# Tile 1 in tile 0's order of columns, another order of the first loads, and B asked earlier

## The reference

```python
w = weights[conditions]                      # per sample 64 x 64
x = x + einsum('bct,bcd->bdt', x, w)         # layer 0, over the channels
H = einsum('btd,od->bto', x, W)              # layer 1, W is 512 x 512
xa = einsum('btd,brd->btr', x, A[idx])       # rank 16, 8 adapters
delta = einsum('btr,bor->bto', xa, B[idx]) * s[idx]
x = x + H + delta
```

## Time and profile before

| | us |
|---|---|
| median of 3 runs (77.91 to 78.04) | 78.03 |
| the profiled execution | 78.45 |
| its span in the trace | 76.8 |
| TensorE busy | 71.4 |
| VectorE, ScalarE, GpSimd busy | 54.9, 51.1, 32.8 |

### The profile page before, as it was taken

One profiled execution on the slowest core, in us unless ns is written; L12 is line 12 of the kernel. 1 busy time (PEld: TensorE's weight loads), 2 busy tenths in 40 slices (PEclk: granted clock), 3 DMA queues, 4 the chain that ended last, 5 costly groups with the idle time before them and its releaser, 6 DMA issues.

```text
span 76.8 us, 1946 instructions
## 1 busy us (share of the span) xinstructions
PE 71.4 (93%) x466; PEld 65.3 (85%) x466; DVE 54.9 (72%) x144; ACT 51.1 (67%) x126; POOL 32.8 (43%) x76
## 2 busy tenths in 40 slices
PE   3996999979999999999999999999999999999940
PEld 3974888938899989999999999999999999999930
DVE  4006985386869887979598877978697959685920
ACT  0586861881997697686768676968678676667430
POOL 5700395095599934545155706570655250000000
PEclk9999999999999999999999999999999999999999
DMA  0899459157689899759956863578407430303025
GB/s 0 211 370 388 149 120 314 44 163 258 197 274 271 292 294 288 247 181 284 331 136 225 273 225 89 168 219 294 162 23 254 137 141 0 137 13 137 0 109 169
DMA packets 10238, 14.56 MB, mean 190 GB/s; under 512 B 3698, under 2 KB 5234, under 8 KB 10226
## 3 DMA queue, kind: packets, MB, share of 16 engines
q1 hardware_dynamic: 7586, 9.04, 36.7%
q0 software_dynamic: 1536, 4.20, 17.6%
q10 hardware_dynamic: 1104, 1.19, 4.9%
HBM read 10.23 MB, written 4.19 MB: 188 GB/s over the span
## 4 chain that ended last, share of the span: by engine, by line
PE 74%; DMA 13%; ACT 2%; DVE 2%; issue 2%; ACTq 2%; POOLq 0%; POOL 0%
PE z_ps L616 53%; DMA w_raw<-w_t 7%; DMA b_raw<-b_t 5%; PE out_ps L658 5%; PE out_ps L671 4%; PE out_ps L672 4%; PE out_ps L676 4%; PE v_ps L650 3%; ACT b_high L345 2%; DVE b_stack L483 1%; ACTq L291 1%; PE out_ps L664 1%; ACT x_high L352 1%; ACTq L295 1%; DVE out_sb L591 1%
## 5 line engine op out<-in xcount | busy, mean ns | idle before, releaser
L616 PE MATMUL z_ps<-moving,x_high 128*128 128x272 f32 x224 | 33.3, 289 | 0.0
L616 PEld LDWEIGHTS z_ps<-moving,x_high 128*128 128x128 f32 x224 | 29.9, 188 | 0.5
L252 POOL DMA_DIRECT2D b_raw<-b_t x32 | 16.1, 505 | 12.8 <-issue 6.2
L616 PE MATMUL z_ps<-moving,x_low 128*128 128x272 f32 x112 | 18.7, 289 | 0.0
L616 PEld LDWEIGHTS z_ps<-moving,x_low 128*128 128x128 f32 x112 | 15.8, 188 | 0.0
L245 POOL CAST moving<-a_table 128x128 fp32r x28 | 8.2, 322 | 15.1 <-PE z_ps L616 14.4
L483 DVE TENSOR_TENSOR b_stack<-b_raw,b_high 128x512 fp32r<-128x512 f32 x16 | 11.7, 734 | 2.2 <-ACT b_high L345 2.2
L474 DVE TENSOR_TENSOR z_low<-z_ps,z_high 128x272 fp32r<-128x272 f32 (+1 forms) x28 | 11.8, 421 | 1.2 <-ACT z_high L329 0.2
L345 ACT ACTIVATE b_high<-b_raw,group_sb 128x512 fp32r<-128x512 f32 x16 | 11.5, 716 | 1.4 <-DMA b_raw<-b_t 1.4
L329 ACT ACTIVATE z_high<-z_ps 128x272 fp32r<-128x272 f32 (+1 forms) x28 | 10.5, 376 | 0.1
L451 DVE TENSOR_TENSOR x_low<-x_raw,x_high 128x512 fp32r<-128x512 f32 x14 | 10.5, 751 | 0.1
(11 more groups left out here) (52 smaller groups left out, 71.1 us busy)
## 6 DMA issues: line engine op xcount, KB each, us to landing
b_raw<-b_t POOLq DMA_DIRECT2D x32, 128.0 KB, 3.3
x_raw<-xt SPq DMA_DIRECT2D x15, 256.0 KB, 4.4
out<-out_sb SPq DMA_DIRECT2D x15, 256.0 KB, 3.0
w_raw<-w_t ACTq DMA_DIRECT2D x2, 272.0 KB, 3.8
w_sb<-w SPq DMA_DIRECT2D x32, 16.0 KB, 3.2
a_scales<-a_t ACTq DMA_DIRECT2D x1, 260.0 KB, 3.9
x_raw<-xt SPq DMA_DIRECT2D x2, 128.0 KB, 3.5
w_raw<-w_t ACTq DMA_DIRECT2D x1, 240.0 KB, 5.7
```

The source lines that it names most:

```text
L252: pool.dma_start(b_raw[s * C:(s + 1) * C, t % BBUFS, :], b_t[ds(which[s], 1), :, :].rearrange("a r (g n) -> (a r) g n", g=1) .to_broadcast ...
L616: last = nc.tensor.matmul(z_bank(t, part), x[:, t % XBUFS, k * P:(k + 1) * P], moving[:, int(n == HL), k, at:at + HALF], start=((n, k) == ...
```

## The change

Tile 1 now uses tile 0's layout (`side(t)` is 0 for both plain tiles): its A columns stand right of W and its A bank is bank 1. The columns right of W in `w_raw` therefore serve tile 0 and then tile 1, and `take_raw_a(1)` waits for tile 0's A bank to be done. TensorE's order becomes tile 0 W, tile 1 W, tile 0 A, two thirds of w_bank(2), weigh_low_rank(0), the last third, tile 1 A, out of tile 0, weigh_low_rank(1), a_bank(2). ScalarE's queue issues W 0, W 1, x(1), A; W piece 2 goes to SyncE's queue in x(1)'s place. GpSimd's first request for B waits for W piece 1 instead of piece 2. On ScalarE and VectorE the order of the steps in the opening follows.

```diff
@@ side and banks
+        def side(t):
+            return 0 if t < PLAIN else t % 2
-            return A_BANK[t % 2] if part == A_PART else 1 - A_BANK[t % 2]
+            return A_BANK[side(t)] if part == A_PART else 1 - A_BANK[side(t)]
...
@@ SyncE
-            load_x(1)
+            load_w(2)
             load_w(3)
             load_x(2)
...
@@ GpSimd
-            pool.wait_ge(w_loaded[2], 16)
+            pool.wait_ge(w_loaded[1], 16)
             load_b(which[0], 0)
...
@@ ScalarE
             load_w(0)
+            load_w(1)
+            act.dma_start(x_raw[:, 1, :], xt[1]).then_inc(x_loaded[1], 16)
             act.dma_start(a_scales[:], a_t).then_inc(a_loaded, 16)
-            load_w(1)
-            load_w(2)
...
-                at = 0 if t % 2 else AC + OUT
+                at = AC + OUT
+                if t:
+                    act.wait_ge(plain_bank_done[t - 1], 1)
...
             high_of_w(0)
-            act.wait_ge(a_loaded, 16)
-            take_raw_a(1)
-            take_raw_a(0)
             high_of_w(1)
             take_z(0, W_PART)
+            act.wait_ge(a_loaded, 16)
+            take_raw_a(0)
             high_of_w(2)
             high_of_x(2)
             high_of_w(3)
+            take_z(1, W_PART)
             act.wait_ge(a_scaled_ready, 1)
             nc.scalar.activation(a_table[:, :, 0, :], a_scaled[:], ACT.Copy).then_inc(a_high_ready, 1)
-            take_z(1, A_PART)
+            take_raw_a(1)
             take_z(0, A_PART)
+            high_of_v(0)
             act.wait_ge(groups_ready, 2)
             high_of_b(0)
+            high_of_z(2, W_PART)
             high_of_x(3)
             high_of_b(1)
-            take_z(1, W_PART)
-            high_of_v(0)
+            take_z(1, A_PART)
+            high_of_w0(BATCH_OF[2])
             high_of_v(1)
-            high_of_z(2, W_PART)
-            high_of_w0(BATCH_OF[2])
+            take_out(0)
...
-            take_out(0)
             take_out(1)
@@ VectorE
+            low_of_x(2)
             low_of_w(2)
-            low_of_x(2)
+            low_of_w(3)
             dve.wait_ge(own_rank_ready, 2 + PER)
-            take_low_rank(1)
-            low_of_w(3)
             take_low_rank(0)
...
+            low_of_v(0)
             low_of_b(0)
+            low_of_z(2, W_PART)
+            take_low_rank(1)
             low_of_b(1)
-            low_of_v(0)
-            low_of_v(1)
-            low_of_z(2, W_PART)
             low_of_x(3)
             low_of_w0(BATCH_OF[2])
+            low_of_v(1)
@@ TensorE
             pe.wait_ge(x_loaded[1], 16)
+            plain_products(1, W_PART, by_row).then_inc(w_bank_done, 1)
             pe.wait_ge(raw_cols_ready, PER)
-            plain_products(1, A_PART, by_row).then_inc(plain_bank_done[1], 1)
-            pe.wait_ge(raw_cols_ready, 2 * PER)
             pe.wait_ge(w_loaded[2], 16)
             plain_products(0, A_PART, by_row[:K // 2])
...
             plain_products(0, A_PART, by_row[-1:]).then_inc(plain_bank_done[0], 1)
-            plain_products(1, W_PART, by_row).then_inc(w_bank_done, 1)
 
             pe.wait_ge(z_plain_ready[0], 1)
             pe.wait_ge(w_low_ready, 2)
-            w_bank(2, 0, K)
+            w_bank(2, 0, 2 * K)
             weigh_low_rank(0)
-            w_bank(2, K, 2 * K)
+            w_bank(2, 2 * K, 3 * K)
+            pe.wait_ge(raw_cols_ready, 2 * PER)
+            plain_products(1, A_PART, by_row).then_inc(plain_bank_done[1], 1)
+            plain_layer0(0)
             weigh_low_rank(1)
-            w_bank(2, 2 * K, 3 * K)
-            plain_layer0(0)
```

8 lines of the change are left out of this document (4 added, 4 removed).

## The result

| | before | changed |
|---|---|---|
| median, 20 runs each, us | 78.55 (77.91 to 79.71) | 78.06 (77.31 to 78.89) |
| the profiled execution | 78.45 | 77.90 |
| its span | 76.8 | 76.2 |
| start of weigh_low_rank(0) (behind one third of w_bank(2) in before, behind two in the changed kernel) | 13.79 | 12.13 |
| end of a_bank(2) | 18.72 | 17.78 |

Changed over before is 0.994, with a 95% interval of 0.9912 to 0.9969: faster by 0.49 us, where 1.21 was forecast. The ratio and its interval leave out the executions that took over 1.5% more than the fastest of their kernel; the medians take in all 20. These runs of before have their median at 78.55 and not at the 78.03 of the first three, so the time to set beside the forecast is the gain, not the 76.8.

What follows compares the result with a forecast made beforehand. TensorE's chain was taken as the bound, through W's and B's transfers before 17.24 us. Ending a_bank(2) at 17.51 instead of 18.72 saves 1.21 us, so 78.03 becomes 76.8 us; forecast 76.5 to 77.1, range with rivals 76.1 to 77.7.

Steps and rivals of the forecast that it cites:

- What bounds the kernel; the head: Opening: TensorE idles 1.46 and 0.91 us before a_bank(2) ends; W's second piece before A gains 1.09 us at third matmul.
- A's columns: After tile 1's W bank: A lands at 8.05, so TensorE waits 0.47 us, from 8.40 to 8.87; bounds 0 and 0.9.
- Part 3: Chain through ScalarE and VectorE to tile 0's mask: TensorE idles 0.32 us; an earlier A lengthens this wait.
- The chain to weigh_low_rank(0): x(2), high, low, two low W pieces, then mask: weigh_low_rank(0) starts at 11.97, within 11.65 to 12.2.
- rival 1: In the head, early B pushes x(2) by 0.65 us: gain 0.6, time 77.4 us; chance 0.14.
- From there to the end of a_bank(2): From weigh_low_rank(0), TensorE needs 5.54 us, no work added or saved, so a_bank(2) ends at 17.51 instead of 18.72.
- The 0.91 of B and v(0) is gone because both are early.: TensorE's 0.91 us idle before tile 0's low-rank product vanishes because SyncE and GpSimd are asked a piece sooner.
- What stays put: After the opening: GpSimd's work for tiles 2 and 3 moves up by up to 0.9 us; nothing lost later.
- rival 2: GpSimd doesn't move, ScalarE waits for the identity of tiles 4 and 5: 0.45 given back, 77.3 us; chance 0.13.
- The signal named for it: Sign listed as proving the forecast wrong: TensorE has gaps between 22 and 27 us; no size given.
- Rivals 4 and 5: Head: B starves A, 78.2 us, chance 0.10 including no change; or x(1) held back, at most 0.3 us, no own chance.
- rival 3: A lands early (7.6), weigh_low_rank(0) at 11.65 or 11.4: gain 1.5 to 1.8, 76.4 us; chance 0.11.

Runs made afterwards that it cites:

- best kernel: Changed kernel with VectorE's mask of tile 0 before its last two low W pieces and B asked at W's third piece: 77.26 us (0.9854), again 77.68 (0.9879).
- the experiment with the old loads: Changed kernel with the first loads issued in the order of the kernel before, all else changed: 78.20 us, 0.9965 of before.
- the kernel with B late: Changed kernel with GpSimd's first request for B waiting for W's third piece again, as in before: 77.74 us, 0.9913 of before.
- the kernel with the casts on purpose: Changed kernel with GpSimd's casts from tile 6 on released just ahead of VectorE's subtraction, to make them collide: 78.13 us, 0.9958 of before.
- the kernel in which GpSimd waits: Changed kernel with GpSimd waiting for VectorE's subtraction of tile 3 before it takes tile 5's A columns: 77.60 us, 0.9907 of before.

## Why the prediction was off, step by step

- **What bounds the kernel; the head.** Right in what it rests on: the second W piece landed at 5.24 (forecast 5.25), the third matmul is at 5.70, as forecast, and from there tile 0's and tile 1's W banks run without a gap. One reading under it is wrong: the first two matmuls of before were not through at 5.33 with 1.46 us lost. Their four records start at 4.43, 5.04, 5.49 and 5.76, since the clock rose only at 5.56; the row itself names 0.63 us of idle time. The 0.449 us for a matmul is the price at full clock alone. The 1.09 us from third matmul to third matmul stand, but for these two executions: in before the W piece came at 6.33 (7.00 and 7.41 in two others of the old order), and in the changed kernel the clock had risen by 4.43. In the best kernel's second profile, where it rose at 7.25, the third matmul starts at 6.49 with nothing but the pace ahead of it. By the medians the experiment with the old loads comes out at 78.20 against 78.06, which is hardly less gain. The sum had no term for the clock.
- **A's columns.** Mis-sized to the good side: A landed at 7.67, not at 8.05, inside the bound "in the middle of its slot". No stall near 8.4; the first products of w_bank(2) start at 10.21 with no idle time. As Part 3 said, the wait moved into the next one.
- **The chain to weigh_low_rank(0).** The mechanism is right to the row (x(2), high, low, two low pieces, mask), the start 0.16 us later than forecast, 12.13 against 11.97. x(2) came 0.27 later than in before (9.13 against 8.86). This is rival 1 in small: GpSimd's early requests take a share from SyncE's queue. It cost 0.3 here, not 0.65, and pushed w0 of tile 0 by 1.2 us as well, which no step of mine had. That stayed hidden behind the mask, until the mask was taken away. That these delays are B's is borne out by the kernel with B late (8.92 and 9.36).
- **From there to the end of a_bank(2).** 5.65 us instead of 5.54. Together with the 0.16 that makes 0.94 instead of 1.21.
- **"The 0.91 of B and v(0) is gone because both are early."** The gap is gone; the reason given is half wrong. With B late it is gone too. The new order alone is enough: v(0) is ahead, and B has its cover without being asked sooner. The early request alone, in the kernel before, closed the gap as well, but by the ratio brought 0.5 us at the very most.
- **What stays put.** The step that failed: it put the loss from a_bank(2) to the end at nothing. GpSimd's work for tiles 2 and 3 did move up, 15.21 to 14.09, so rival 2 didn't come, and its casts for tile 5 by 1.63. I asked only whether GpSimd would be late. That it could be in the way, by working while VectorE has a short instruction on the path, was nowhere in the sum or in the rivals. The sum's "to the end, where TensorE runs without a gap" was off by 0.65 us in this profile: 0.55 of idle ahead of weigh_low_rank(3), and 0.11 in which that product, behind the idle time, takes 0.39 in the chain against 0.28 before.
- **The signal named for it.** "Wrong if TensorE has gaps between 22 and 27 us" is what came.
- **The rivals.** Rivals 4 and 5 didn't come. Of rival 3 the condition came (A at 7.67), but not the gain: the chain by x(2) held weigh_low_rank(0) at 12.13, not 11.65. The time is outside the range of 76.1 to 77.7. A part of that is the base: 78.03 is at the low end of this kernel's runs. On the base of the comparison, 78.55, the forecast would be 77.3, still 0.7 below. The steps above account for the 0.7 in the two profiles; how it divides in an ordinary run, between the meeting at tile 3, the landings and the clock, isn't shown.

**Open.** Why in the changed kernel VectorE is held through the casts and on through the addition behind them. 0.08 us behind a cast's start it was held, 0.17 us behind it was not; what decides between is not tried. Why the clock rises at 4.25 us in one execution and at 7.25 in another, and how often it is late in the runs without a profile. And so how much the order of the loads brings in an ordinary run: the profiles mix it with both that and the landings.

## What to carry to other kernels

When an opening is shortened, look at what the moved engines will run beside, and not only at whether they are in time: a short VectorE instruction with two SBUF operands, on the path, next to GpSimd work that became free to run sooner. Ask for data sooner only if something waits for it; here the early request pushed x(2) and w0, and taking it back while putting the mask first gave a kernel 0.43 us faster than the changed one. Where removing a releaser gains nothing, look for the one right behind it and take both away: each edit left TensorE at 12.03, and the two together brought 11.48. And before two openings are compared by one profile each, look when the spacing of the matmuls halves: here that moved the same work by up to 1.0 us.

## What the runs showed of the hardware

- A VectorE subtraction of 0.22 us took 0.54 in all five tiles where a GpSimd addition of 0.73 had begun 0.27 us before it, ending 0.08 us behind it. One that reads PSUM kept its 0.41 us beside such an addition (z_low, in the kernel with the casts on purpose).
- Started 0.08 us behind a cast that an addition follows, it took 1.00 to 1.23 us in four profiles, and ended 0.08 or 0.09 behind the addition. Started 0.17 behind the cast, it took 0.22, addition or not. Started 0.07 behind a cast with one more cast and no addition to follow (tile 4 of the kernel in which GpSimd waits, at 25.97), it took 0.32.
- TensorE's clock rises from its lower level to its upper one once, between 4.25 and about 7.3 us, at a moment that differs between executions of one program (4.43 and 5.89, 4.93 and 7.25). The matmul records of the first banks are 0.45 us apart before it and 0.23 behind it. In two profiles of one program the late rise moved weigh_low_rank(0) from 11.48 to 12.45. The views print a granted clock of 1.00 for the time before the first record.
- Requests on GpSimd's queue push those of SyncE's: x(2) to landing took 5.7 us with B late and 6.0 and 6.4 in the changed kernel. The Trainium skill ("DMA: Bandwidth & Descriptors", Queues, rings and completion order) has each DMA engine go round between all queues with work, and for GpSimd's queue the traces agree.
- The landing of the same request differs between executions: the second W piece, third on ScalarE's queue, at 6.33, 7.00 and 7.41.
